# Moving a transposing DMA and the low parts it carries from the end of a step to its front, on SyncE and GpSimd

## The reference, cut to what matters

```python
q = heads(hidden_states @ W_q)
probs_t = softmax(einsum('bhsd,bhtd->bhst', q, k_t) * scale)          # text, 73 columns
text_out = einsum('bhst,bhtd->bhsd', probs_t, v_t)
attn_scores = einsum('bhsd,bhnd->bhsn', q, k_ip) * scale              # ip, 4 columns
qsem = l2norm(einsum('bhst,bte->bhse', probs_t, text_ehs))
sem = einsum('bhse,bne->bhsn', qsem, l2norm(ip_ehs))
probs_ip = softmax(attn_scores + 0.5 * sem) * spatial_mask
ip_out = einsum('bhsn,bhnd->bhsd', probs_ip, v_ip)
out = (text_out + ip_out) @ W_out + b_out + hidden_states
```

## Time and profile before

| | |
|---|---|
| median of 3 runs | 1106.82 us |
| the profiled execution | 1100.87 us |
| its span | 1098.7 us |
| mean granted clock of TensorE | 0.974 |
| busy share: TensorE, VectorE, ScalarE, GpSimd | 91%, 74%, 62%, 54% |
| DMA, main queue, share of 16 engines | 79.3% |
| matmuls of L1061 in the chain that ended last | 21% of the span |

### The profile page before, as it was taken

How to read it: one execution, slowest core, us unless ns; L and a number is a source line. 1 busy time by engine, 2 the same in 40 slices (tenths; PEclk the granted TensorE clock), 3 DMA queues, 4 the chain that set the end, 5 groups by cost and what they waited for, 6 DMA issues and landing times.

```text
span 1098.7 us, 23677 instructions
## 1 busy us (share of the span) xinstructions
PE 1002.7 (91%) x7637; PEld 807.8 (74%) x7637; DVE 811.6 (74%) x2397; ACT 676.4 (62%) x1995; POOL 590.4 (54%) x1570
## 2 busy tenths in 40 slices
PE   6996687799999999999999999999999999999868
PEld 4872566588777878787777788787878787877745
DVE  3146279778787888788878788788888787878762
ACT  1124377866766767666767667676767667767630
POOL 0000356746666656666556656566656666656550
PEclk9799799999999999999999999999999999999989
DMA  9498568868889888888889888788898889776842
GB/s 289 128 195 211 126 126 168 160 132 169 162 178 184 173 172 176 163 156 184 152 168 178 176 173 160 156 163 164 169 190 180 168 170 184 138 156 115 165 106 91
DMA packets 484393, 180.56 MB, mean 164 GB/s; under 512 B 451228, under 2 KB 462334, under 8 KB 484271
## 3 DMA queue, kind: packets, MB, share of 16 engines
q1 hardware_dynamic: 484271, 179.07, 79.3%
HBM read 42.74 MB, written 27.22 MB: 64 GB/s over the span
## 4 chain that ended last, share of the span: by engine, by line
PE 61%; DMA 7%; DVE 5%; SPq 5%; issue 4%; ACT 4%; POOL 3%; POOLq 0%; DVEq 0%; ACTq 0%
PE ps_O L1061 21%; PE ps_Q L1095 19%; PE ps_S L1034 10%; PE ps_U L1081 9%; DMA ipT<-ip 4%; DMA pts<-ph 3%; SPq L734 3%; ACT pr L818 2%; PE ps_M L1109 2%; POOL ph L902 2%; SPq L745 1%; ACT ph L830 1%; DVE pr L972 1%; SPq L706 1%; DVE n L984 1%
## 5 line engine op out<-in xcount | busy, mean ns | idle before, releaser
L818 ACT ACTIVATE pr<-ps_S,bias 128x73 f32<-128x73 f32 x1280 | 288.7, 337 | 138.1 <-DVE bias L939 138.1
L902 POOL TENSOR_TENSOR ph<-pr,ph 128x440 f16<-128x440 f32 x320 | 227.6, 732 | 205.3 <-ACT ph L830 205.1
L1061 PE MATMUL ps_O<-wo_hi,aT 128*128 128x320 f16 x1280 | 299.1, 305 | 35.6 <-DMA ipT<-ip 21.1
L1095 PE MATMUL ps_Q<-xT,wq_hi 128*128 128x512 f32 x800 | 278.7, 413 | 7.7 <-DVE qT L909 6.8
L830 ACT ACTIVATE ph<-pr 128x584 f16<-128x584 f32 x320 | 204.2, 688 | 5.1
L1061 PEld LDWEIGHTS ps_O<-wo_hi,aT 128*128 128x128 f16 x1280 | 126.6, 99 | 96.7 <-issue 35.9
L1061 PE MATMUL ps_O<-wo_lo,aT 128*128 128x320 f16 x640 | 194.3, 304 | 0.0
L1081 PE MATMUL ps_U<-xm,pts 128*128 128x110 f16 (+1 forms) x2560 | 157.2, 213 | 18.9 <-DMA pts<-ph 14.5
L1034 PE MATMUL ps_S<-kbd,qT 128*128 128x308 f32 x960 | 170.3, 313 | 3.5 <-ACT pr L818 3.2
L1081 PEld LDWEIGHTS ps_U<-xm,pts 128*128 128x128 f16 (+1 forms) x2560 | 144.5, 98 | 36.9 <-DMA pts<-ph 15.0
L1095 PEld LDWEIGHTS ps_Q<-xT,wq_hi 128*128 128x128 f32 x800 | 145.2, 190 | 35.5 <-DVE qT L909 8.7
(11 more groups left out here) (175 smaller groups left out, 1310.8 us busy)
## 6 DMA issues: line engine op xcount, KB each, us to landing
out_dram<-x_in SPq DMA_DIRECT2D x64, 320.0 KB, 2.9
x_in<-in_x_dram SPq DMA_DIRECT2D x60, 320.0 KB, 3.4
w_k<-in_L_xattn_W_k_dram SPq DMA_DIRECT2D x5, 512.0 KB, 9.2
w_ip<-in_L_xattn_W_k_ip_dram SPq DMA_DIRECT2D x1, 2560.0 KB, 12.0
w_v<-in_L_xattn_W_v_dram SPq DMA_DIRECT2D x1, 2560.0 KB, 19.9
w_ip<-in_L_xattn_W_v_ip_dram SPq DMA_DIRECT2D x1, 2560.0 KB, 10.9
pts<-ph SPq DMA_TRANSPOSE x160, 4.4
xm<-x_d SPq DMA_DIRECT2D x20, 110.0 KB
```

The lines of the kernel that those rows point to most:

```text
L818: last = nc.scalar.activation(pr[p % P_RING][:, j, h, :], sc[:, j, h, 0:T], ACT.Exp, bias=bias[p % 2][:, j, h:h + 1], scale=SCALE)
L902: nc.gpsimd.tensor_tensor(lo, full[:, :, t0:t1], one[:, :, 0, t0:t1], ALU.subtract).then_inc(pl_ready, 1)
L1061: last = nc.tensor.matmul(o_bank[half % 2][:, 0:HALF], stationary, moving, start=(k, a, b_) == O_MMS[0], stop=(k, a, b_) == O_MMS[-1])
L1095: last = nc.tensor.matmul(ps_Q[:], wq[a][:, c, k * P:(k + 1) * P], xT[(CC * i + c) % XT_RING][b_][:], start=(c, a, b_) == Q_MMS[0], stop=( ...
```

## The change

In the step that `ip_at` picks out, SyncE's block with the waits and the issue of `ipT` moves from behind `aT` to ahead of `pts(p)`; the step's loads and stores stay ahead of it. GpSimd's block with the wait for `ip_hi` and the two subtractions of L895 moves to the front of its step, ahead of the Newton steps (there are none in such a step), the low part of `at16` and the rest. The text of both blocks is the same as before.

```diff
@@ SyncE, in the loop over p
+                i = ip_at(p)
+                if i is not None:
+
+                    sp.wait_ge(ip_hi, i + 1)
+                    sp.wait_ge(ip_lo, 2 * (i + 1))
+                    if i >= IT_RING:
+                        sp.wait_ge(o_ready, OUTS * (i - IT_RING + 1))
+                    sp.dma_start_transpose(ipT[i % IT_RING][:], ip16[:].rearrange("p s k c -> p (s k c)")
+                                           ).then_inc(ipT_loaded[i % IT_RING], 16)
                 if pair_of(p) is not None:
 
                     sp.wait_ge(ph_ready, p + 1)
@@ behind the issue of aT
-                i = ip_at(p)
-                if i is not None:
-                    ... (the same lines)
@@ GpSimd, in the loop over p
             for p in range(FIRST, LAST):
+                i = ip_at(p)
+                if i is not None:
+
+                    pool.wait_ge(ip_hi, i + 1)
+                    hi = ip16[:, :, 0, 0:IPR]
+                    for lo, c0, c1 in ((ip16[:, :, 0, IPR:P], 0, IP_LO), (ip16[:, :, 1, 0:IPR - IP_LO], IP_LO, IPR)):
+                        nc.gpsimd.tensor_tensor(lo, pip[:, :, c0:c1], hi[:, :, c0:c1], ALU.subtract).then_inc(ip_lo, 1)
                 n = slot_of(p - 4)
```

## The result

The changed kernel took 1066.78 us (median of 4 runs, 1065.55 to 1074.3) beside 1107.89 us for the kernel before (4 runs): ratio 0.9643, 95% interval 0.9595 to 0.9691. It is faster, as forecast, but by 41 us (40 from the 1106.82 that the forecast started from) where 27.4 were forecast, and 1066.8 lies under the range's low end of 1072. Two later sets of the same kernel on other occasions gave 1069.0 and 1071.66 us against 1103.54 and 1102.2 for before (ratios 0.9687, 0.9658 to 0.9717, and 0.9711, 0.9677 to 0.9744). So the change is worth about 3% (2.9 and 3.1% by the later sets), and the first comparison was at the favourable end.

The account below looks back on a forecast made before the run. TensorE, 91% busy, was taken as the bound: 31.3 us of ipT stalls plus 4.9 of clock, less 8.2 and 0.6 for pts, gives 27.4 us. Forecast about 1073.5, as a median 1079.4 us; range 1072 to 1092.

Parts of the forecast that it names:

- from the sum to the time: Whole kernel: 27.4 us off the profiled 1100.87 gives about 1073.5 us, then 1079.4 as a median.
- pts(6): Transpose for the pair after the changed step: its later use waits in six tiles, giving back 8.2 us.
- the carry-over: Whole kernel: the 6 us between before's profiled execution and its median of 1106.82 were added to the changed kernel's time.
- The stall goes completely: TensorE's wait for ipT at L1061 in 15 of 16 tiles vanishes, 31.3 us; about 4 us of cover in tile 5.
- GpSimd's move costs nothing: The two earlier subtractions cost 0, hidden by 1.26 us of idle time; without that cover 0.94 us.
- pts(5) is held up: Transpose of the changed step, now behind ipT on SyncE: loss of 0 to 1.2 us, 0.6 taken.
- rival 1: SyncE's DMAs: ipT ahead delays pts(5), aT and pts(6) by 1.27 us; gain 16.3, time 1090.5 us; chance 0.17.
- The clock term: TensorE's clock drops after stalls in tiles 0, 6 and 8 vanish: 1.63 us each, 4.9 us, bounds 0 and 4.9.
- The sum for the stretch: Main loop between scores of pairs 15 and 158: forecast gain 27.4 us, or 29.2 without tile 14's 1.8.
- Rivals 1 to 3: Besides rival 1: ipT lands no earlier, 1106.8 us, chance 0.04; SyncE's queue never recovers before pts(6), 1112 us, chance 0.04.

Follow-up runs that it names:

- pool_only: Kernel before with only GpSimd's block moved to the front of its step, SyncE as before: 1102.41 us, ratio 0.9988.
- sp_only: Kernel before with only SyncE's ipT block moved ahead of pts(p), GpSimd as before: 1071.24 us, ratio 0.9697.
- a_again: The changed kernel with no edit, profiled a second time and timed again: 1069.0 us (6 runs).

## Why the prediction was right in its mechanism and wrong in its size

The step that failed is the last one, from the sum to the time. It is 12.6 us off (1079.4 against 1066.8). The 6 us between before's profiled execution and its median were carried over to the changed kernel, whose own offset is 1.0: 4.9 us of the miss. The prologue and the tail were put at nothing, and measured 1.7 and 3.3. A term of the sum was mis-sized too, pts(6): 8.2 us, measured 5.3. Its 1.8 us for tile 14 fall behind pair 158, so what the sum forecast for the stretch is 29.2 us, and 30.1 were measured. The miss is then 0.9 in the stretch, 5.1 behind it, 1.7 ahead of it and 4.9 in the carry-over. How much of it is luck the repeats tell: by the two later sets the medians are 34.5 and 30.5 us apart, not 41.

- *The stall goes completely.* Right: 0 in tiles 0 to 14 in all three profiles of the changed kernel, 31.3 us. ipT's landing became a little longer (3.6 us in the median, 5.4 at most, from 3.2 and 3.8), which the cover took.
- *GpSimd's move costs nothing.* Right, and it gives nothing (pool_only).
- *pts(5) is held up: 0 to 1.2 us, 0.6 taken.* It cost 0: no wait at pts(5) in the changed kernel. It did go out later against its scores where SyncE has no hole, by 1.8, 1.1 and 1.9 us in tiles 2, 6 and 10, and there 0.9 to 1.4 us between landing and use were left. From issue to landing it took 4.7 us in the median of 15 tiles against 4.8 before. The rule behind rival 1 (the Trainium skill, DMA: Bandwidth & Descriptors, "Two DMAs through the same engine are not ordered": descriptors of one queue of a DMA engine start in order) costs nothing here; the landings show no added queueing.
- *pts(6) takes back 8.2 us in six tiles.* This term was mis-sized. Its waits in the changed kernel are 0.93, 3.26, 0.97 and 1.06 us (tiles 2, 6, 10, 14), 6.2 in sum, 0.9 of which before had too. The excess is 1.7 us in tile 14, 0.9 in tile 10, 0.6 in tile 3 and 0.3 each in tiles 0 and 2; tile 6 lost 0.8 more than forecast. What failed is that I kept pts(6)'s landings as they were in before. They come sooner once ipT is at the front: 4.31 to 4.35 us in the median of 15 tiles in the eight profiles with that order, 4.71 to 4.97 in the six others. In tile 3 it is 4.3 to 4.4 against 4.9 to 6.0 (6.0 in before, which I used), and tile 3 waits for nothing; in tile 14 it was 5.1 in the changed kernel against 6.0, and its wait grew by 0.15 where I had 1.81. Why the landing shortens no run isolates. All waits for pts in the stretch grew by 6.0 us (5.7 to 11.7).
- *The clock term, 4.9 us.* TensorE's busy time in the stretch fell by 5.3 us between the two first profiles (798.4 to 793.0, above). But falls are not a fixed three: the profiles of before have three and four, the changed kernel's one and two, and a new long wait can bring one back: all three profiles of the changed kernel have one behind pts(6) of tile 6 (0.56 above), while sp_only, which waits 2.7 us there, has none.
- *The sum for the stretch*: 29.2 forecast (27.4 without tile 14's 1.8), 30.1 measured, 29.5 in the mean of the repeats. The stalls' 31.3 and the 5.3 of busy time less the 6.0 of new waits for pts make 30.6; small waits that grew by 0.5 are the rest.
- *The carry-over to the median failed.* I added before's offset of 6 us between profiled execution and median to the changed kernel. The changed kernel's medians lie 1.0 and, for a_again, 0.1 us above their profiled executions, and over 57 later runs before's median is 1102 to 1104. This is 5 of the 12.6 us by which the time was missed.
- *The tail and the prologue had no term.* 3.3 and 1.7 us by the first two profiles, both within what one kernel shows from execution to execution (58.6 against 55.4; 201.6 to 203.7). The range allowed 1.5 us for the scatter of executions. The repeats show 1065.6 to 1074.3 for the changed kernel and 1096.7 to 1111.6 for before, so a median of three or four carries some 2 to 3 us by itself (an estimate from this scatter).

Rivals 1 to 3 are out: pts waits stayed at 14 us, ipT's went, and pts(6) was not issued later against its step (8.1 us behind its pair's scores in the median, 8.0 before; only tile 6 is 0.8 later).

## What to carry to other kernels

A DMA whose data is long ready can stall the busiest engine just by its place in an ordered issue list; look at what stands between "source ready" and "issued", and move it ahead of the first entry that has to wait for something anyway. What such a move gives is the stall less the smallest distance between landing and use of what was started before the stall; that distance is itself an estimate, for the landings can change with the order (pts(6) came 0.4 us sooner here). Before you carry a sum from a profile over to a median, ask whether the offset belongs to the kernel or to a few runs.

## What the runs showed that I had not expected

The granted clock fell behind idle times of 2 us in one execution and not behind ones of 2.4 us in the same, and the tail of the same kernel had three falls in one execution and none in two others. A fall behind a stall cost some 1.6 us in the earlier trace rows, and the two profiles of before have five and seven in and behind the stretch: by this estimate falls make several of the microseconds by which its executions differ.
